# A four-layer transformer on one core: ScalarE takes the first bfloat16 copy of the last 16 features from VectorE

## The reference

```python
shift1, scale1, gate1, shift2, scale2, gate2 = split(silu(c) @ ada_w + ada_b, 6)
h = norm(x) * (1 + scale1) + shift1          # "h1" in the kernel
x = x + gate1 * (attention(h @ qkv_w + qkv_b, heads=16) @ proj_w + proj_b)
h = norm(x) * (1 + scale2) + shift2          # "h2" in the kernel
x = x + gate2 * (gelu(h @ fc1_w + fc1_b) @ fc2_w + fc2_b)
```

## Time and profile before

| | |
|---|---|
| median of 3 runs | 1380.3 us (1373.98 to 1381.52) |
| the profiled execution | 1377.49 us, span of its instructions 1375.8 us |
| TensorE busy (matmul) | 1213.0 us, 88% of the span |
| VectorE busy | 1065.6 us, 77% |
| ScalarE busy | 881.2 us, 64% |
| GpSimd busy | 260.8 us, 19% |
| mean granted TensorE clock | 0.980 of full speed |

### The profile page before, as it was taken

One profiled execution on the slowest core, in us unless ns is written; L12 is line 12 of the kernel. 1 busy time (PEld: TensorE's weight loads), 2 busy tenths in 40 slices (PEclk: granted clock), 3 DMA queues, 4 the chain that ended last, 5 costly groups with the idle time before them and its releaser, 6 DMA issues.

```text
span 1375.8 us, 36470 instructions
## 1 busy us (share of the span) xinstructions
PE 1213.0 (88%) x13028; PEld 768.5 (56%) x13060; DVE 1065.6 (77%) x2814; ACT 881.2 (64%) x2122; POOL 260.8 (19%) x382
## 2 busy tenths in 40 slices
PE   6775779999969999999999999999989999998886
PEld 4312345565536666666666666666655665666654
DVE  5467678898868888888888888888878888897632
ACT  1132566676757777777777777777777666766653
POOL 3010011221122222222122221222212222211101
PEclk9999899999989999999999999999999999999998
DMA  6431355433464444444444444444578767667410
GB/s 174 129 96 44 100 125 129 109 87 93 110 174 130 123 130 124 121 124 125 125 124 127 124 124 125 126 125 129 128 151 151 146 142 130 121 129 149 78 27 26
DMA packets 209409, 163.63 MB, mean 119 GB/s; under 512 B 82872, under 2 KB 187264, under 8 KB 209232
## 3 DMA queue, kind: packets, MB, share of 16 engines
q1 hardware_dynamic: 204928, 158.94, 48.2%
q10 hardware_dynamic: 4304, 2.36, 0.6%
HBM read 98.05 MB, written 62.41 MB: 117 GB/s over the span
## 4 chain that ended last, share of the span: by engine, by line
PE 50%; DVE 25%; issue 10%; ACT 7%; SPq 4%; DMA 3%; another core or an unknown queue 0%; DVEq 0%; POOLq 0%; POOL 0%; ACTq 0%
PE lin L1630 10%; DVE maxima L1181 8%; PE lin L1646 7%; PE o_bank L1583 6%; PE score_bank L1476 5%; PE score_bank L1520 3%; PE st_bank L1551 3%; ACT h2T L773 2%; DVE stats L1043 2%; PE lin L1634 2%; PE lin L1616 2%; ACT p_room L787 2%; PE score_bank L1492 2%; DVE gated L1239 2%; PE score_bank L1486 1%
## 5 line engine op out<-in xcount | busy, mean ns | idle before, releaser
L1181 DVE TENSOR_REDUCE maxima<-score_bank 128x4 f32<-128x512 f32 x512 | 328.6, 683 | 61.8 <-PE score_bank L1520 59.2
L787 ACT ACTIVATE p_room<-st_bank 128x512 f32<-128x512 f32 x512 | 276.7, 596 | 108.7 <-PE st_bank L1551 74.8
L689 POOL TENSOR_TENSOR part_low<-qk_rest,part_mid 96x512 bf16<-96x512 f32 x96 | 113.8, 1186 | 403.6 <-DVE part_mid L1164 403.6
L1630 PE MATMUL lin<-h2T,w_h 128*128 128x512 f32 (+1 forms) x320 | 170.1, 630 | 4.4 <-ACT h2T L773 2.6
L1646 PE MATMUL lin<-w_f,gelu 128*128 128x144 f32 (+1 forms) x1280 | 170.0, 288 | 0.8 <-DVE gated L1239 0.8
L1583 PE MATMUL o_bank<-p_room,v_room 128*32 128x128 f32 x4096 | 166.1, 280 | 0.0
L1646 PEld LDWEIGHTS lin<-w_f,gelu 128*128 128x128 f32 (+1 forms) x1280 | 160.5, 190 | 2.8 <-DVE gated L1239 1.6
L1520 PE MATMUL score_bank<-stack_room 62*128 62x128 bf16 x2048 | 103.7, 221 | 56.2 <-DVE maxima L1181 21.5
L893 ACT ACTIVATE gelu<-lin 128x512 f32<-128x512 f32 (+1 forms) x160 | 90.9, 589 | 81.9 <-PE lin L1634 75.5
L1520 PEld LDWEIGHTS score_bank<-stack_room 62*128 62x128 bf16 x2048 | 59.8, 95 | 129.9 <-issue 53.3
L680 POOL TENSOR_TENSOR x<-x,gated 128x288 f32<-128x288 f32 x64 | 53.9, 842 | 403.1 <-DVE gated L1239 403.1
(11 more groups left out here) (176 smaller groups left out, 2182.8 us busy)
## 6 DMA issues: line engine op xcount, KB each, us to landing
stack_room<-stack_dram SPq DMA_DIRECT2D x192, 256.0 KB, 5.8
stack_dram<-part_high SPq DMA_DIRECT2D x64, 288.0 KB, 3.5
gates<-gates_dram SPq DMA_DIRECT2D x64, 288.0 KB, 3.4
norm_room<-stack_dram SPq DMA_DIRECT2D x64, 256.0 KB, 6.1
stack_dram<-part_mid SPq DMA_DIRECT2D x64, 192.0 KB, 2.5
stack_dram<-part_high SPq DMA_DIRECT2D x64, 144.0 KB, 3.3
stack_dram<-part_mid SPq DMA_DIRECT2D x64, 96.0 KB, 3.0
stack_dram<-part_low SPq DMA_DIRECT2D x64, 96.0 KB, 2.1
```

Of the source, the lines that this page charges most:

```text
L689: eng.tensor_tensor(part_low[:, T, :], qk_rest[:, T, :], part_mid[:, T, :], ALU.subtract)\
L787: eng.activation(probs[:, i % PBUFS, :], st_bank[i % 2][:, :], ACT.Exp, scale=float(HD) ** -0.5)\
L1181: eng.tensor_reduce(maxima[:, b, CH * c:CH * c + CH], bank_of(f"S{i}")[:, :].rearrange("p (h k) -> p h k", h=CH), AX_X, ALU.max)\
L1630: eng.matmul(o, w_h[l][:, cols], h2T[:, :], start=True, stop=False)
```

## The change

The cast L1094 goes from VectorE to ScalarE. It is placed in `modulated`, for the second half only (h = 1), between the two `hT_last` pieces and the two `h1T` / `h2T` pieces. It covers all four sequences of the group, and waits for ScalarE's own sixth `h1_ready` / `h2_ready`, that is for the `hT_last` piece just ahead of it. VectorE's `last_parts` now begins with a wait for it.

```diff
@@ modulated (ScalarE)
                     eng.activation(columns_of(hT_last[i], flow, b), tokens_of(bank[0:REM_ROWS, c + TOK:c + 256], flow), ACT.Identity,
                                    bias=mods_rem[i][:, 0, b:b + 1], scale=mods_rem[i][:, 1, b:b + 1])\
                        .then_inc(S[("h1_ready", "h2_ready")[i]], 1)
+                if h == 1:
+
+                    need(eng, ("h1_ready", "h2_ready")[i], g, 5)
+                    rem = (h1T_rem[g % H1_BUFS], h2T_rem)[i]
+                    eng.activation(rem[0:REM_ROWS, :], hT_last[i][:, :], ACT.Copy)\
+                       .then_inc(S[("h1_parts", "h2_parts")[i]], 1)
                 for b in (2 * h, 2 * h + 1):
@@ last_parts (VectorE)
                 done = ("h1_parts", "h2_parts")[i]
                 rem = (h1T_rem[g % H1_BUFS], h2T_rem)[i]
-                need(eng, ("h1_ready", "h2_ready")[i], g, 5)
-                if i == 0:
-                    need(eng, "v_done", g - H1_BUFS, 1)
-                else:
-
-                    need(eng, "fc1_done", g - 1, FCT - 1)
-                eng.tensor_copy(rem[0:REM_ROWS, :], hT_last[i][:, :]).then_inc(S[done], 1)
                 need(eng, done, g, 0)
```

## The result

The changed kernel takes 1424.25 us (median of 4 runs, 1413.21 to 1428.99), the kernel before beside it 1380.91 us: a ratio of 1.031, 95% interval 1.0254 to 1.037, so 43 us slower. The four runs of the changed kernel lie 16 us apart, so a difference of some 8 us between two medians of four is not clear of noise by itself. The forecast was 1409, its range ended at 1422. The profiled execution of the changed kernel took 1424.8 us.

What follows compares the result with a forecast made beforehand. In layers 2 and 3 it took TensorE, released by ScalarE's last pieces, as the bound. Terms 12.1 + 10.9 + 3.0 + 3.7 + 2.7 - 2.8 + 0.9 = +30.5 us gave 1409 us, range 1394 to 1422.

Steps and rivals of the forecast that it cites:

- The delay at a place, 0.67 us: On ScalarE, the copy makes the last h1T or h2T piece come 0.67 us later (bounds 0.50 to 0.77).
- The tie at L1531: At the h1 place TensorE starts 0.15 us behind the last h1T piece, so the delay there counts, with nil slack.
- rival 1: Only the h2 places pay, h1's delay being swallowed by an unseen wait: +16.6 us, about 1396 us; chance 0.14.
- Layers 2 and 3, +23.0: Later pieces delay TensorE: 18 h2 places cost +12.1 us and 17 h1 places +10.9 us.
- Layer 4, +6.7: Six h1 places cost +3.0 us and six h2 places, where TensorE waits for h2T, +3.7 us.
- The tail, +2.7: Four h2 places at the end, all on the chain of waits, cost +2.7 us.
- Layer 1, -2.8: VectorE bounds here, so losing the h1 cast gains 0.46 us at each of 6 places: -2.8 us.
- The h2 term of +0.9: Layer 1: an estimated 0.9 us added for two early h2 places with little slack.
- VectorE's wait at the h1 place, 1.35 forecast: In layers 2 and 3, VectorE's wait for TensorE's L1646 would grow from 0.22 to about 1.35 us.
- The step that failed: In layers 2 and 3 TensorE's granted clock was 1.00 despite many short waits, so clock loss was given little weight.
- rival 4: More than forecast: ScalarE's self-wait costs 0.2 us or more (+8 us), or TensorE's clock drops to 1.2 GHz; chance 0.06.

Runs made afterwards that it cites:

- e1: Changed kernel, but only h1's copy goes to ScalarE and h2's cast stays on VectorE: 1399.0 us, ratio 1.012.
- e2: Changed kernel, but only h2's copy goes to ScalarE and h1's cast stays on VectorE: 1400.8 us, ratio 1.013.
- e10: Changed kernel plus unread matmuls, ten before TensorE's h1-place wait and six before the maxima wait ahead, last groups too: 1410.95 us, ratio 1.021.
- e3: Kernel before, VectorE keeping both casts, with ScalarE making the same copy as well into a spare tile nobody reads: 1429.1 us, ratio 1.033.
- e4: Changed kernel plus ten small unread matmuls before TensorE's wait at the h1 place, from layer 2 on: 1416.3 us, ratio 1.024.
- e8: Changed kernel plus ten small unread matmuls before TensorE's wait for h2T, none at the h1 place: 1424.2 us, ratio 1.031.
- e5: Changed kernel with all 64 ScalarE copies moved behind ScalarE's copy of the values: 1380.89 us, ratio 1.000.
- e6: Changed kernel with the ScalarE copies moved directly behind the two late pieces of h1T and h2T: 1394.1 us, ratio 1.009.
- e7: Kernel before, with ScalarE copying behind the pieces at the h1 place of layers 1 and 4 alone: 1377.9 us, ratio 0.997.
- e9: Kernel before plus ten small unread matmuls before TensorE's wait at the h1 place: 1390.6 us, ratio 1.005.
- e11: The same kernel as e7, timed again with more rounds: 1378.86 us, ratio 0.9984.

## Why the prediction missed, by its own steps

- **The delay at a place, 0.67 us: right.** The copy takes 0.629 us (0.63 taken), its wait 0.03 (0.04); e1 and e2 measure 0.65 and 0.66 a period. The hundredth is luck: at the h1 place the overlaps are 0.18 in front and 0.09 behind where the sum took 0.14 for both, so the pair starts 0.75 later, and the pair, taken as unchanged, is 0.08 shorter.
- **The tie at L1531 (rival 1): right to dismiss it.** The h1 place pays in full (e1). At 1396 us rival 1 priced what e2 measures as 1400.8.
- **Layers 2 and 3, +23.0:** the waits give 625.0 - 603.3 = 21.7 (e10). Measured in the changed kernel is 28.3; four stretches are the other 6.6, and the sum had nothing for them.
- **Layer 4, +6.7:** e10 has 7.8 with one stretch in it, so about 6.1 from the waits. Measured is 16.9; the six further stretches are 9.1.
- **The tail, +2.7: probably too small.** Six kernels with late `h2T` (changed, e2, e3, e4, e8, e10) have 145.2 to 148.4 us there, seven without (before, e1, e5, e6, e7, e9, e11) 139.3 to 145.6: 4.2 more in the mean. Both kinds have half-clock stretches in the tail, and these alone may move it: e7 and e11 are one kernel, and have 142.2 us with 16 at half clock and 145.6 with 30. How much of the excess is the clock I didn't separate.
- **Layer 1, -2.8:** 0.34 a group and not 0.46, so about -2.0. The h2 term of +0.9 was not tested by itself; in e2, which moves that copy alone, the four periods up to the first border take 179.3 us, 0.3 more than before.
- **VectorE's wait at the h1 place, 1.35 forecast, 1.09 found.** By the timelines the maxima that stand ahead start 1.74 us behind the first `hT_last` where it was 1.61, and `h_rest` starts 0.12 us later behind them than the cast did; nothing hangs on it.
- **The step that failed** is the one that left TensorE's clock out of the sum: "In layers 2 and 3 the granted clock is 1.00 with many short waits, so I give it little." It took the clock for robust because it had been at 1.00 in the earlier trace rows. But it was at 1.00 with one wait of about half a microsecond at the h1 place (for the maxima), and the change puts a second one right behind it. What the runs showed in its place is that these two waits together were followed by 3.4 us at half clock in 4 of the 17 groups of layers 2 and 3 and in all six of layer 4, at 1.67 us each in layers 2 and 3. This was part of rival 4, with a chance of 0.06 and no price of its own. Its worth is 13.3 us by the medians (1424.25 less e10's 1410.95), and at e10 the kernel stands at 28.9 us above before by the medians, where the sum said 30.5. That these agree to 1.6 us is partly luck: by the profiled executions it is 34.6 us, with 7.2 of them in the tail.

That the clock is what the 13 us are is shown for layers 2 to 4 by e4, e8, e9 and e10 together. Left open: why only some of the groups of layers 2 and 3 fall (in the changed kernel every second one up to 647 us and then none, though the same two waits stand in each), and so how many stretches another kernel with such waits would have.

## What to carry to other kernels

Price a moved instruction by what stands directly behind it on its new engine, not by that engine's busy share: the same 64 copies cost 43 us in front of the pieces that release a bank, 13 us directly behind these and nothing behind the values. When a change adds waits to TensorE, look at what idle time already stands beside the new wait, and give the loss of clock there a price of its own (here 1.67 us for each 3.4 us at half clock). If waits can't be avoided, a few matmuls whose result nobody reads, put exactly into the wait, can be worth their place, and cost time where there is no wait.

## What the runs showed that I had not expected

- Waits of 0.50 and 0.76 us, with TensorE busy 2.16 us of the 3.50 ahead, were followed by 3.4 us at a granted clock of 0.52, and the same pair, with as much busy time ahead, by none in the next group; a wait of 1.1 us alone, at the h2 place (e2), in 17 groups by none.
- A kernel with ten (e4) or sixteen (e10) more matmuls a group ran 8 and 13 us faster than the same kernel without.
- An instruction on ScalarE that waits for ScalarE's own last result started 0.03 us behind it, and the one behind the copy still started 0.09 us before the copy ended: such a wait costs the overlap of 0.14 to 0.18 us and little more.
